# Eight chained layers on one core: three reduced-precision passes in two attentions, rows staged an item ahead, row scatters paced, expert loads and some steps moved

## The reference

```python
x = _layernorm(x + L0_attn(x))   # Mamba-2: h = rmsnorm(x); proj = h @ in_proj; conv of 4 taps, silu;
                                 # chunked scan with 4 heads, state 128; x + (y * silu(gate)) @ out_proj
x = _layernorm(x + L0_ffn(x))    # silu(x @ Wgate_int8 * s) * (x @ Wup_int8 * s) @ Wdown_int8 * s
x = _layernorm(x + L1_attn(x))   # softmax attention, 16 heads of 128
x = _layernorm(x + L1_ffn(x))    # top 4 of 32 experts of 96, plus 16 small experts of 128
x = _layernorm(x + L2_attn(x))   # Mamba selective scan, 512 channels, state 16
x = _layernorm(x + L2_ffn(x))    # ternary weights, width 1024, an RMS norm in between
x = _layernorm(x + L3_attn(x))   # 16 heads of 16 over one shared k, v; then gelu(h @ wfc) @ wproj, width 1024
x = _layernorm(x + L3_ffn(x))    # width 688, with LoRA terms shared and of 2 of 8 routed experts
```

## Time and profile before

| | us |
|---|---|
| median of three runs (2622.68 to 2630.52) | 2625.47 |
| the profiled execution | 2626.96 |
| its span in the profile | 2625.2 |
| l0_attn | 4 to 263 |
| l0_ffn | 264 to 399 |
| l1_attn | 400 to 949 |
| l1_ffn | 953 to 1268 |
| l2_attn | 1268 to 1865 |
| l2_ffn | 1870 to 2012 |
| l3_attn | 2012 to 2402 |
| l3_ffn | 2403 to 2617 |

### The profile page before, as it was taken

The page is one execution under the profiler, slowest core; times in us unless marked ns, Lnnn a source line. Parts: engine busy times, 40 slices in busy tenths (PEclk is TensorE's granted clock), DMA queues, the critical chain, the costliest instruction groups (busy, mean ns, idle before and its releaser), DMA issues. The chain is left out here.

```text
span 2625.2 us, 46486 instructions
## 1 busy us (share of the span) xinstructions
PE 2266.9 (86%) x15909; PEld 1960.0 (75%) x15909; DVE 1695.8 (65%) x4076; ACT 1450.6 (55%) x3780; POOL 797.3 (30%) x810
## 2 busy tenths in 40 slices
PE   6998877999999948999569888899696899997997
PEld 5776877999999937999447666677586576766886
DVE  4676676877777773553278887778364666663443
ACT  4664446877777723333367777776242666663332
POOL 1211110011111120000467887768485222221000
PEclk9888889999999978999779999999797999998999
DMA  5000111000000263333321111000300000000000
GB/s 145 1 1 1 42 56 33 2 17 17 17 18 17 79 211 103 123 110 98 118 72 49 49 50 44 23 36 11 115 1 1 1 1 1 1 1 1 1 1 33
DMA packets 73611, 111.70 MB, mean 43 GB/s; under 512 B 15674, under 2 KB 59315, under 8 KB 72005
## 3 DMA queue, kind: packets, MB, share of 16 engines
q1 hardware_dynamic: 63828, 86.18, 10.3%
q0 software_dynamic: 7488, 21.50, 2.5%
q10 hardware_dynamic: 2064, 1.05, 0.2%
HBM read 79.73 MB, written 28.97 MB: 41 GB/s over the span
## 5 line engine op out<-in xcount | busy, mean ns | idle before, releaser
L1848 POOL TENSOR_TENSOR l2a_hb<-l2a_hb,l2a_Cb 128x1024 f32<-128x1024 f32 x128 | 303.0, 2378 | 118.4 <-DVE l2a_hb L2329 117.5
L2329 DVE TENSOR_TENSOR_SCAN l2a_hb<-l2a_dA,l2a_dB 128x1024 f32<-128x1024 f32 x128 | 289.3, 2277 | 69.9 <-PE l2a_dB L1935 25.6
L2170 ACT ACTIVATE l2a_dA<-l2a_delta,l2a_An 128x255 f32<-128x255 f32 x512 | 214.6, 499 | 25.5 <-DVE l2a_delta L2258 13.8
L1935 PE MATMUL l2a_dB<-l2a_diag,l2a_dxT 64*128 64x128 f32 x2048 | 188.0, 305 | 25.9 <-DVE l2a_hb L2329 13.2
L1935 PEld LDWEIGHTS l2a_dB<-l2a_diag,l2a_dxT 64*128 64x128 f32 x2048 | 139.2, 193 | 89.6 <-PE l2a_dB L1935 37.1
L895 PE MATMUL l1a_QK<-l1a_xh,early_wqkv_h 128*128 128x256 f32 x512 | 148.7, 290 | 2.3 <-DVE l1a_xl L128 1.5
L895 PE MATMUL l1a_QK<-l1a_xl,early_wqkv_h 128*128 128x256 f32 x512 | 145.9, 285 | 0.4 <-issue 0.4
L895 PE MATMUL l1a_QK<-l1a_xh,early_wqkv 128*128 128x256 f32 x512 | 145.9, 285 | 0.4 <-issue 0.4
L1148 ACT ACTIVATE l1a_ex<-l1a_S,l1a_nm 128x256 f32<-128x256 f32 x256 | 119.3, 471 | 44.9 <-DVE l1a_nm L1200 43.2
L1955 PE MATMUL l2a_YS<-ident,l2a_hb 128*128 128x128 f32 x1024 | 140.3, 283 | 1.0 <-POOL l2a_hb L1848 1.0
L1183 DVE TENSOR_TENSOR l1a_qkl<-l1a_QK,l1a_qkh 128x512 fp32r<-128x512 f32 x128 | 88.0, 688 | 56.2 <-ACT l1a_qkh L1123 35.9
(11 more groups left out here) (682 smaller groups left out, 7473.5 us busy)
## 6 DMA issues: line engine op xcount, KB each, us to landing
l2a_Cb<-c_rows SPq DMA_DIRECT2D x8, 2048.0 KB
l1f_xl<-moe_x_rows SPq DMA_DIRECT2D x95, 128.0 KB, 2.1
moe_y_rows<-l1f_yo SPq DMA_DIRECT2D x95, 128.0 KB, 1.7
first_raw<-in_L_attn_w_qkv_dram SPq DMA_DIRECT2D x18, 256.0 KB, 2.9
moe_x_rows<-X SPq DMA_DIRECT2D x1, 4224.0 KB, 19.4
l1f_dL<-in_L_ffn_Wd_dram SPq DMA_DIRECT2D x1, 3072.0 KB
routes_over_low<-in_L_ffn_Wu_dram SPq DMA_DIRECT2D x2, 1056.0 KB
X<-in_L_attn_x_dram SPq DMA_DIRECT2D x8, 256.0 KB, 6.0
```

What stands on the lines that cost most here:

```text
L1848: nc.gpsimd.tensor_tensor(h[:, :, :], h[:, :, :], Cb[p][:, s0:s0 + UN, :], ALU.mult).then_inc(hc_ready, 1)
L1935: last = nc.tensor.matmul(out[:, m:m + 2, j * P + a:j * P + a + HP], dxT[q][a:a + HP, j, c * P:(c + 1) * P], diag[q][a:a + HP, j, s0 + m:s ...
L2170: last = nc.scalar.activation(dA[(i * NU + u) % DAS][:, n, 1:SEQ], delta[q][:, c, 1:SEQ], ACT.Exp, scale=An[:, c, s0 + n:s0 + n + 1])
L2329: nc.vector.tensor_tensor_scan(flat(hb[u % RING]), flat(dA[(i * NU + u) % DAS]), dB[u % 2][:, :], 0.0, ALU.mult, ALU.add).then_inc(scanned, 1)
```

## The change

In l0_attn the products of items 1 and up (all items for the out-projection) use `product`; GpSimd splits the weights once and the rows of each item (`split_x`), ScalarE and VectorE split `yg`. The first tap of the convolution moves from VectorE to ScalarE (`first_taps`), `log_dt` goes behind the gate's silu, the norm and transpose of rows i + 2 are done in item i, and PE starts when the input weights are there. In l0_ffn GpSimd does rstd an item later. In l1_attn each scatter waits until a head's q and k are there (heads 9 to 16), and SyncE loads more of Wu, and the small experts' down weights. l1_ffn has these loads no longer. l2_ffn sums squares at f = 4. l3_attn's products of `wo`, `wfc` and `wproj` use `product`: in item 0 VectorE forms the low parts of the weights between its softmax blocks, GpSimd splits `h2T` and copies the high part of `a`, VectorE subtracts. In l3_ffn ScalarE's scores come behind the copy `hh`, and VectorE's routing is in two steps. Buffers, semaphore names and the same lines in prologues and epilogues are left out here.

```diff
--- before.py
+++ after.py
@@ -249,14 +253,16 @@
-for b in range(1, ITEMS):
+sp.dma_start(sh.X[:, 1], sh.x_dram[:, 1]).then_inc(x_next, 16)
+for b in range(2, ITEMS):
...
-sp.dma_start(wo[:, :, :], w["L0_attn_out_proj_w"].rearrange("(k p) n -> p k n", p=P)).then_inc(w_loaded, 16)
+sp.dma_start(wo[:, :, :], w["L0_attn_out_proj_w"].rearrange("(k p) n -> p k n", p=P)).then_inc(wo_loaded, 16)
...
-sp.wait_ge(w_loaded, 32)
-sp.wait_ge(sh.x_rest, 16 * (ITEMS - 1))
+sp.wait_ge(wo_loaded, 16)
+sp.wait_ge(x_next, 16)
+sp.wait_ge(sh.x_rest, 16 * (ITEMS - 2))
@@ -284,15 +290,34 @@
+def split(whole, high, low, loaded, n):
+    pool.wait_ge(loaded, 16)
+    nc.gpsimd.tensor_copy(high[:, :, :], whole[:, :, :]).then_inc(w_high, 1)
+    pool.wait_ge(w_high, n + 1)
+    nc.gpsimd.tensor_tensor(low[:, :, :], whole[:, :, :], high[:, :, :].bitcast(F32), ALU.subtract).then_inc(w_low, 1)
...
+split(wi, wih, wil, w_loaded, 0)
+split(wo, woh, wol, wo_loaded, 1)
...
+def split_x(k, q):
...
+    pool.wait_ge(ph.xT_ready, k + 1)
+    pool.wait_ge(gate_ready, (k - 1) * NT)
+    nc.gpsimd.tensor_copy(xh[q][:, :, :], ph.xT[q][:, :, :]).then_inc(x_high, 1)
+    pool.wait_ge(x_high, k)
+    nc.gpsimd.tensor_tensor(xl[q][:, :, :], ph.xT[q][:, :, :], xh[q][:, :, :].bitcast(F32), ALU.subtract).then_inc(x_low, 1)
...
+    if left > 1:
+        inverse_rms(pool, i + 2)
...
-        inverse_rms(pool, i + 2)
+        split_x(i + 2, p)
@@ -321,23 +347,28 @@
+def project(out, cols, k, q):
...
+    if k:
+        return product(nc.tensor, out, [(wih[:, kc, cols], wil[:, kc, cols], xh[q][:, kc, :], xl[q][:, kc, :])
+                                        for kc in range(KC)])
+    for kc in range(KC):
+        last = nc.tensor.matmul(out, wi[:, kc, cols], ph.xT[q][:, kc, :], start=(kc == 0), stop=(kc == KC - 1))
+    return last
...
+    if k and half == 0:
+        pe.wait_ge(x_low, k)
...
-        for kc in range(KC):
-            last = nc.tensor.matmul(W[half][:, f % 2 * SEQ:(f % 2 + 1) * SEQ],
-                                    wi[:, kc, DI + f * P:DI + (f + 1) * P], ph.xT[q][:, kc, :],
-                                    start=(kc == 0), stop=(kc == KC - 1))
+        last = project(W[half][:, f % 2 * SEQ:(f % 2 + 1) * SEQ], slice(DI + f * P, DI + (f + 1) * P), k, q)
...
-        for kc in range(KC):
-            last = nc.tensor.matmul(W[2][:, n * SEQ:(n + 1) * SEQ],
-                                    wi[:, kc, 2 * DI + NH + n * NS:2 * DI + NH + (n + 1) * NS], ph.xT[q][:, kc, :],
-                                    start=(kc == 0), stop=(kc == KC - 1))
+        last = project(W[2][:, n * SEQ:(n + 1) * SEQ], slice(2 * DI + NH + n * NS, 2 * DI + NH + (n + 1) * NS), k, q)
@@ -393,10 +422,17 @@
+if left:
+    pe.wait_ge(ph.xT_ready, i + 2)
...
-    for kc in range(KC):
-        last = nc.tensor.matmul(bank[:, :], ph.xT[p][:, kc, j * P:(j + 1) * P], wi[:, kc, 0:DI],
-                                start=(kc == 0), stop=(kc == KC - 1))
+    rows = slice(j * P, (j + 1) * P)
+    if i:
+        last = product(nc.tensor, bank[:, :], [(xh[p][:, kc, rows], xl[p][:, kc, rows], wih[:, kc, 0:DI], wil[:, kc, 0:DI])
+                                               for kc in range(KC)])
+    else:
+        for kc in range(KC):
+            last = nc.tensor.matmul(bank[:, :], ph.xT[p][:, kc, rows], wi[:, kc, 0:DI],
+                                    start=(kc == 0), stop=(kc == KC - 1))
@@ -410,6 +446,9 @@
+if left > 1:
+    pe.wait_ge(sg_ready, i * NT + 1)
+    turn(ph, pe, i + 2)
@@ -417,23 +456,27 @@
+    if i == 0:
+        pe.wait_ge(w_low, 2)
...
+        cols = slice(j * D, (j + 1) * D)
...
-        for f in range(FC):
-            last = nc.tensor.matmul(ph.Y[:, j * D:(j + 1) * D], ygT[:, j, f, :], wo[:, f, :],
-                                    start=(f == 0), stop=(f == FC - 1))
+        product(nc.tensor, ph.Y[:, cols], [(ygh[:, j, f, :], None, woh[:, f, :], wol[:, f, :]) for f in range(FC)], last=False)
+        pe.wait_ge(yT_low, i * NT + j + 1)
+        last = product(nc.tensor, ph.Y[:, cols], [(None, ygl[:, j, f, :], woh[:, f, :], None) for f in range(FC)], first=False)
...
-pe.wait_ge(w_loaded, 32)
-pe.wait_ge(masks_ready, 6)
+pe.wait_ge(w_loaded, 16)
...
+turn_la(0)
...
-turn_la(0)
+turn(ph, pe, 1)
+pe.wait_ge(masks_ready, 6)
@@ -467,6 +510,13 @@
+def first_taps(k):
+    act.wait_ge(xs_ready, k * FC)
+    for f in range(FC):
+        act.wait_ge(ssm_ready, k * FC + (f // 2 + 1) * 2)
+        nc.scalar.activation(cv[:, f, :], W[f // 2][:, f % 2 * SEQ:(f % 2 + 1) * SEQ], ACT.Copy,
+                             scale=cw[:, CONV - 1, f:f + 1]).then_inc(tap_ready, 1)
@@ -512,37 +560,45 @@
-        log_dt(i + 1)
+        first_taps(i + 1)
...
-        squares(act, i + 2)
+        stage_scaled(act, i + 2)
...
+        log_dt(i + 1)
...
+    if left > 1:
+        keep_scaled(act, i + 2, p)
...
-    if left > 1:
-        stage_scaled(act, i + 2)
...
+    if i + 3 < ITEMS:
+        squares(act, i + 3)
...
+act.wait_ge(sh.x_loaded, 16)
...
-act.wait_ge(sh.x_rest, 16 * (ITEMS - 1))
-squares(act, 1)
...
+first_taps(0)
+act.wait_ge(x_next, 16)
+squares(act, 1)
...
+stage_scaled(act, 1)
+keep_scaled(act, 1, 1)
...
-stage_scaled(act, 1)
+act.wait_ge(sh.x_rest, 16 * (ITEMS - 2))
+squares(act, 2)
@@ -671,7 +724,7 @@
-convolve(i + 1, (0, 1))
+convolve(i + 1, (1, 2))
@@ -683,17 +736,19 @@
+    for j in range(NT):
+        dve.wait_ge(yT_kept, i * NT + j + 1)
+        nc.vector.tensor_tensor(ygl[:, j, :, :].rearrange("p f t -> p (f t)"), W[4 + j][:, :],
+                                ygh[:, j, :, :].rearrange("p f t -> p (f t)").bitcast(F32), ALU.subtract).then_inc(yT_low, 1)
+    if left:
...
-        convolve(i + 1, (2, 3))
+        convolve(i + 1, (3,))
...
-    if left > 1:
-        mean_squares(dve, i + 2)
...
-mean_squares(dve, 1)
@@ -702,10 +757,11 @@
-convolve(0, (0, 1))
...
+mean_squares(dve, 1)
+convolve(0, (1, 2))
...
-convolve(0, (2, 3))
+convolve(0, (3,))
@@ -758,8 +814,8 @@
-if not first:
-    rstd(ph, pool, i - 1)
+if i >= 2:
+    rstd(ph, pool, i - 2)
@@ -985,8 +1042,14 @@
+sp.wait_ge(vc_ready, (ITEMS - 1) * NH + NH // 2)
+routes.load(sp, ((0, some), (part, part + some), (2 * part, 2 * part + some)))
+routes.load_small_down(sp, 0, NH // 2)
...
+sp.wait_ge(vc_ready, ITEMS * NH)
+routes.load(sp, ((0, 3 * part),))
+routes.load_small_down(sp, NH // 2, NH)
@@ -1022,7 +1085,7 @@
-scatter(nc, pool, sh, i - 2, j)
+scatter(nc, pool, sh, i - 2, j, qk_ready, i * NH + 9 + j * routes.TOPK)
@@ -1253,10 +1316,12 @@
-def scatter(nc, pool, sh, i, j):
+def scatter(nc, pool, sh, i, j, pace=None, begun=0):
...
+        if pace is not None:
+            pool.wait_ge(pace, begun + k)
@@ -1355,14 +1420,11 @@
-small_down = lambda kc: w["L1_ffn_cWd"].rearrange("i e (k c) -> k i e c", k=KC)[kc]
...
-    routes.load(sp, ((0, sh.early.columns),))
...
-    sp.dma_start(dS[:, :, 0, :], small_down(0)).then_inc(routes.small_down_loaded, 16)
@@ -2493,7 +2554,7 @@
-if f == 2 and not first:
+if f == 4 and not first:
@@ -2689,6 +2760,24 @@
+for whole, high, _, n in WEIGHTS:
+    nc.gpsimd.tensor_copy(part(high, n), part(whole, n)).then_inc(w_high, 1)
...
+def split_h2(k):
...
+    pool.wait_ge(h2T_ready, (k + 1) * KC)
+    pool.wait_ge(fc_ready, k * (FC // 2))
+    nc.gpsimd.tensor_copy(flat(h2h[:, :, :]), flat(h2T[:, :, :])).then_inc(h2_high, 1)
+    pool.wait_ge(h2_high, k + 1)
+    nc.gpsimd.tensor_tensor(flat(h2l[:, :, :]), flat(h2T[:, :, :]), flat(h2h[:, :, :]).bitcast(F32), ALU.subtract
+                            ).then_inc(h2_low, 1)
...
+def high_a(k):
...
+    pool.wait_ge(ph.y_ready, k)
+    for m in range(FC // 2):
+        pool.wait_ge(gelu_ready, k * FC + (m + 1) * 2)
+        nc.gpsimd.tensor_copy(part(ah, m), part(a, m)).then_inc(a_high, 1)
@@ -2710,7 +2799,11 @@
+if not first:
+    split_h2(i - 1)
...
+if not first:
+    high_a(i - 1)
@@ -2761,25 +2856,33 @@
+if m == 0:
+    pe.wait_ge(h2_low, k + 1)
+    if k == 0:
+        pe.wait_ge(w_low, WFC_LOW)
...
-    for kc in range(KC):
-        last = nc.tensor.matmul(FB[m % 2][:, n * SEQ:(n + 1) * SEQ], wfc[:, kc, f * P:(f + 1) * P],
-                                h2T[:, kc, :], start=(kc == 0), stop=(kc == KC - 1))
+    cols = slice(f * P, (f + 1) * P)
+    last = product(nc.tensor, FB[m % 2][:, n * SEQ:(n + 1) * SEQ],
+                   [(wfch[:, kc, cols], wfcl[:, kc, cols], h2h[:, kc, :], h2l[:, kc, :]) for kc in range(KC)])
...
-        pe.wait_ge(gelu_ready, (k + 1) * FC)
...
+        if k == 0:
+            pe.wait_ge(w_low, WPR_LOW)
...
-    for f in range(half * FC // 2, (half + 1) * FC // 2):
-        last = nc.tensor.matmul(ph.Y[:, j * D:(j + 1) * D], a[:, f, j * P:(j + 1) * P], wpr[:, f, :],
-                                start=(f == 0), stop=(f == FC - 1))
+    rows = slice(j * P, (j + 1) * P)
+    if j == 0:
+        pe.wait_ge(a_low, k * (FC // 2) + (half + 1) * FC // 4)
+    last = product(nc.tensor, ph.Y[:, j * D:(j + 1) * D],
```

(44 more changed lines are left out.)

81 lines of the change are left out of this document (45 added, 36 removed).

## The result

The changed kernel takes 2565.31 us (median of four runs, 2563.47 to 2567.45), the kernel before 2627.99 beside it: ratio 0.9771, 95% interval 0.9753 to 0.9788. That is 62.7 us less; the sum said 74 less, 2553. The total lies in the range. Two of its terms do not: l0_attn (9.0 for at least 10) and l2_ffn (nothing for at least 2) gave less than they were priced at. l1_ffn gave less too, but inside its range; l0_ffn and l1_attn gave more, 8.4 us together, and this offset part of the shortfall by luck.

What follows compares the result with a forecast made beforehand. PE, busy 86% of the span, led, with bounds differing by phase; l0_attn −22, l0_ffn −4, l1_attn −26, l1_ffn −13, l2_ffn −6, l3_attn −2, l3_ffn −1 sum to −74 on 2627.0: 2553 us, range 2518 to 2597.

Steps and rivals of the forecast that it cites:

- Rival B: l1_attn: a stall belongs to each scatter whenever it comes, so the phase gains 0: 2579 us; chance 0.2.
- Rival E: l1_attn: spread scatters stall a pair of engines 2.68 us each, +102 us, total 2681; chance 0.04.
- takes some 13.9 (my estimate): l0_ffn: VectorE with its handovers to ScalarE takes some 13.9 us an item, so a steady item gains 0.4.
- the phase is short of GpSimd as well, so half returns: l2_ffn: of 13.4 us of waits for squares' sums half comes back, −6 us (−2 to −9).
- both lie in its idle 4.8 us before the silu: l0_attn: ScalarE's taps (4 × 0.42) and fourth table load of 1.28 us fit its idle time.
- GpSimd's 13 us of weight splits fit ahead of item 1's products, with a us or two of lateness I don't charge: l0_attn's start: GpSimd has time to split the weights before item 1 needs them, at no charged cost.
- rival C: GpSimd's new work in l3_attn and l0_attn holds VectorE, costing 14 us: 2567, or 2581 if doubled; chance 0.15.
- PE alone would allow 23.3: l0_attn: with 4.0 us less of products and waits, PE's own loop would take 23.3 us an item.
- my two loops of 23.3 and 23.7: l0_attn: PE's loop of 23.3 us and that through VectorE and ScalarE of 23.7; with one us added, 24.8 an item.
- the loop through VectorE and ScalarE: l0_attn: last tap to shares 3.65, decays 5.15, VectorE 15.2, less 1.66, plus 1.38: 23.7 us an item.
- A: Whole kernel: the summed terms come as priced, 2553 us, holding 2540 to 2570; chance 0.5.
- D: PE's loop sets l0_attn at 23.3 us, l3_attn keeps 2.8 an item, bursts return all 32: 2525; chance 0.1.

Runs made afterwards that it cites:

- e4: Changed kernel with the eight row scatters of an item of l1_attn in a burst again, the paced wait taken out: 2593.13 us, ratio 0.9894.
- e10: Changed kernel with l2_ffn's staging copy of the next rows made by ScalarE in place of GpSimd: ratio 0.9757 to the kernel before.
- e2: Changed kernel with silu's table in l0_attn loaded before ScalarE waits for the last convolution tap: 2562.98 us, ratio 0.9787.
- e1: Changed kernel with GpSimd's weight splits in l0_attn put ahead of the inverse norm of item 1: 2555.90 us, ratio 0.9748.
- e5: Changed kernel, l0_attn: weight splits first, silu table ahead, GpSimd's row split behind the running sums: 2553.19 us, ratio 0.9843, before 2597.22 on that chip.
- e6: Changed kernel with l3_attn as in the kernel before and l2_ffn's squares at f = 2: 2568.03 us, ratio 0.9799.

## Why the prediction was right, and where not

**l1_attn, right.** Rival B, a stall that belongs to each scatter, would have left 68 us an item; they are 62.2. Rival E, 2.68 us for each of 48, falls with it. What a scatter costs beside full engines, alone or one of three, is nothing that shows. I took 26 of a bound of 35; e4 gives 29.

**l1_ffn, right,** with the bound seen in advance, VectorE's routing; 2 of the 13 are lost ahead of it. No run moves the loads back, so this rests on the timeline alone.

**l0_ffn, mis-sized.** The length was right: "takes some 13.9 (my estimate)", and an item is 13.9. That VectorE sets it isn't shown: VectorE is busy 11.8 to 12.1 us of it and PE 12.1 to 12.2, and no run tests it. But I took the gain from the window of one item, 14.8, where the mean of seven was 15.0 with two long stalls, and then half of it: 1.1 us an item were there, not 0.4.

**l2_ffn, wrong step:** "the phase is short of GpSimd as well, so half returns". Nothing returned: the wait changed its name from squares to the staging (13.4 us to 12.5, without the first item's 10.6), both of them waits for GpSimd. e10, which takes an instruction from GpSimd, gets 0.4 to 0.7 us an item.

**l0_attn, the failed term.** −22 was forecast, −9.0 came. The start was to give 5 us and took 2.5 (item 0 ends at 70.6, before at 68.1). The seven distances were to give 17.5 and gave 11.5, and 6.7 of these come from items 2 to 5, whose distances of 28.8 to 30.2 us before the forecast hadn't looked at; where it had looked it got 0.6 and 0.3 for 2.5. Four steps of it.

First "both lie in its idle 4.8 us before the silu". In this trace the table load comes behind the wait of the instruction that needs it, after 4.29 us of idling, and not inside them. By e2 some 0.3 to 0.7 us of it counted.

Second "GpSimd's 13 us of weight splits fit ahead of item 1's products, with a us or two of lateness I don't charge". They did fit (they take 11.3); what they cost is VectorE, held some 9 us at the start, and the rows' split costs it 1 us an item. Of these e1 returns 3.6 to 6.0. I had the row for it, and used it as rival C with 0.42 us in 1.42 as a mean share. This case's rows bear out the Trainium skill, "SBUF — State Buffer", section "Who interferes with whom", which makes it an exclusive lock for the whole instruction: L674 ended 0.05 us after the GpSimd subtraction. In place of a share I should have looked for what VectorE runs beside a GpSimd operation of 5.6 us.

Third, and the largest, "PE alone would allow 23.3": the sum of three passes at mixed clock, 2.8 us of PE's time less. I charged the clock as it was (one group at half) and left it there. In the changed kernel the mean clock of an item fell from 0.87 to 0.81, which is some 10 us at half clock, and PE's busy time fell by 1.0 to 1.4 us and not 2.8. Where the clock was 0.93 (e5) items of three passes took 23.6 to 23.8 us, near my two loops of 23.3 and 23.7. What exactly sets the clock is not shown, nor whether it lengthens the item or a longer chain lowers it.

Fourth, the loop through VectorE and ScalarE was cut short. From the copied shares to the last masked matrices the sum has 5.15 us, the decays alone, though its own rows have 104.71 − 96.25 = 8.46 there. The changed kernel has 8.17 (ScalarE's copies of transposed rows, exp's table load of 1.28 and a wait for PE of 0.72 beside the decays). With it the loop comes to 26.8 us and not 23.7, and the item is 26.96. In e5, at the higher clock and with the silu's table loaded ahead, the stretch is 6.43 and the item 23.6.

That whole f32 then has a mean item of 24.8, my number, is chance: it is made of distances of 24.0 to 24.3 at full clock, two of 28.1 and 26.6 at a lower one, and a last of 22.4. So all of the phase's gain is in the other moves, which no run takes apart (rows staged ahead, first tap on ScalarE, `log_dt` later, the new start), and the three passes took 18.5 to 20.9 us of it back.

**l3_attn, right in sum,** and the prices as well: the steady items are 43.2 us apart, before 44.2 (I had read 44.7), a gain of 1.0 for a forecast of 0.9; VectorE's 0.69 × 9 in item 0 are there, and the hold by GpSimd too. With the old text e6 has 390.0 us for 387.4 to 387.9. Rows answering to the earlier trace rows; the small L3205 takes 1.13 us and ends 0.03 after GpSimd's L2787:

```profile
2189.22 1.13 DVE L3205 TENSOR_SCALAR l3a_nm<-l3a_mx 128x4 f32<-128x4 f32 x1
...
2189.04 1.28 POOL L2787 TENSOR_TENSOR l3a_xr<-X,l3a_r 128x512 f32<-128x512 f32 x1
```

**Rivals.** A happened, less well than summed: its terms missed by 22 us one way and by 9 the other. C's 2567 is the nearest to 2565.3, by luck: most of its 14 us were to be lost in l3_attn, which came out as forecast. It had the right mechanism; its place was l0_attn's start. D's "PE loop decides" named the engine and not the clock.

## What to carry to other kernels

Three cheap products for one dear one gave 1.0 us an item in l3_attn and cost 18.5 to 20.9 us in l0_attn, where their splits lie on a chain beside a nearly full PE and the clock fell with them. So try the order change alone first. Cost a long GpSimd operation by its whole length at whatever VectorE runs beside it. And where a wait for an engine goes and another for the same engine comes, the order is worth nothing: take an instruction from that engine. Look at the items one by one, each with its clock; their mean hid both the miss and its cause here.

## What the hardware showed unexpectedly

A VectorE scan of 64 numbers took 4.77 us in place of 0.18 beside a GpSimd subtraction; a copy in SBUF, which reads one operand there, was held too, by a cast (0.95 us for 0.18) and by a subtraction (1.17), while a scan that reads one operand from PSUM (L671) took its usual 0.67 beside the same subtraction. Eight indirect transfers one after another cost an item of l1_attn some 5 us; the same eight, three in a row and five at 3 to 4.7 us, nothing. One chip ran the kernel before in 2597 us where two others took 2622 to 2628; why is open.
